# Attention output read back with channels on partitions, and the two norms after it on pairs of tiles

## The reference

```
out = softmax(q k^T / 4) v                 # per head; reshaped to 4096 x 256
y   = out @ Wo.T + bo
x2  = x + layernorm(y)
xn2 = layernorm(x2)                        # mean and variance over 256 channels, eps 1e-5
d2  = sum(xn2^2) + sum(centroid^2) - 2 xn2 @ centroid.T    # 8 experts
w, sel = top_k(sqrt(d2), 2); w = softmax(w)
```

## Time and profile before

| | us |
|---|---|
| median of 3 runs | 1725.83 (1725.29 to 1733.98) |
| the profiled execution, whole | 1724.6 |
| its span, first to last instruction | 1722.8 |
| output stage, 871.8 to 1008.3 | 136.5 |
| routing and start of the experts, 1008.3 to 1061.2 | 52.9 |

### The profile page before, as it was taken

How to read it: one execution, slowest core, us unless ns; L and a number is a source line. 1 busy time by engine, 2 the same in 40 slices (tenths; PEclk the granted TensorE clock), 3 DMA queues, 4 the chain that set the end, 5 groups by cost and what they waited for, 6 DMA issues and landing times.

```text
span 1722.8 us, 33008 instructions
## 1 busy us (share of the span) xinstructions
PE 1522.0 (88%) x9922; PEld 865.8 (50%) x9923; DVE 1204.5 (70%) x2083; ACT 886.8 (51%) x1828; POOL 333.1 (19%) x411
## 2 busy tenths in 40 slices
PE   6887999999999999999988935999999999999900
PEld 3554333333333333333356723777777777777700
DVE  7998989999999999999024666444444444445426
ACT  2333058888888888888845732222222222222226
POOL 5665100000000000000011213222222222222204
PEclk9998579999999999999978956999999999999955
DMA  4474704434444433330533371011011011011072
GB/s 131 133 202 141 135 8 91 104 76 81 67 83 67 99 62 83 58 74 15 162 114 112 120 258 42 31 33 33 30 33 33 30 33 33 30 33 33 27 250 98
DMA packets 113495, 141.44 MB, mean 82 GB/s; under 512 B 36057, under 2 KB 86978, under 8 KB 113410
## 3 DMA queue, kind: packets, MB, share of 16 engines
q1 hardware_dynamic: 106594, 121.68, 28.1%
q0 software_dynamic: 6816, 18.62, 3.3%
HBM read 90.46 MB, written 49.81 MB: 81 GB/s over the span
## 4 chain that ended last, share of the span: by engine, by line
PE 73%; DVE 5%; ACT 3%; DMA 3%; issue 3%; SPq 2%; DVEq 0%; POOL 0%; ACTq 0%; POOLq 0%
PE psum L1449 19%; PE psum L1303 18%; PE psum L1329 16%; PE psum L1468 11%; PE psum L1459 3%; DMA weights<-ot_scr 2%; PE psum L1315 2%; DVE mx L813 2%; ACT work L1145 1%; PE psum L1393 1%; ACT weights L1155 1%; SPq L582 1%; PE psum L1435 1%; PE psum L1378 1%; PE psum L1391 1%
## 5 line engine op out<-in xcount | busy, mean ns | idle before, releaser
L813 DVE TENSOR_REDUCE mx<-psum 128x1 f32<-128x1024 f32 x512 | 625.1, 1222 | 22.4 <-PE psum L1303 18.7
L1145 ACT ACTIVATE work<-psum 128x512 f32<-128x512 f32 x1024 | 556.7, 597 | 131.6 <-PE psum L1315 68.4
L1303 PE MATMUL psum<-stack 48*128 48x512 f32 x1024 | 395.8, 470 | 5.6 <-DVE mx L813 3.7
L1315 PE MATMUL psum<-stack 50*128 50x512 f32 x1024 | 377.3, 448 | 0.0
L1449 PE MATMUL psum<-weights,values 128*128 x1136 | 340.8, 453 | 0.6 <-DVE values L1011 0.6
L1329 PE MATMUL psum<-work,values 128*32 128x256 f32 x4096 | 328.9, 393 | 9.2 <-ACT weights L1155 9.2
L1303 PEld LDWEIGHTS psum<-stack 48*128 48x128 f32 x1024 | 160.8, 197 | 231.0 <-DVE mx L813 199.1
L1449 PEld LDWEIGHTS psum<-weights,values 128*128 128x128 f32 x1136 | 211.2, 191 | 99.5 <-issue 3.0
L1221 ACT ACTIVATE values<-values 128x342 f32<-128x342 f32 x142 | 69.3, 488 | 252.9 <-DVE values L1021 252.9
L1468 PE MATMUL psum<-weights,work 114*128 (+1 forms) x852 | 195.9, 379 | 0.8 <-ACT work L1231 0.8
L1329 PEld LDWEIGHTS psum<-work,values 128*32 128x32 f32 x4096 | 82.1, 108 | 197.5 <-ACT work L1145 102.0
(11 more groups left out here) (173 smaller groups left out, 1425.8 us busy)
## 6 DMA issues: line engine op xcount, KB each, us to landing
stack<-qk_scr SPq DMA_DIRECT2D x192, 128.0 KB, 6.5
qk_scr<-weights SPq DMA_DIRECT2D x8, 2048.0 KB, 7.1
weights<-in_w SPq DMA_DIRECT2D x8, 1368.0 KB, 6.1
ot_scr<-weights SPq DMA_DIRECT2D x16, 512.0 KB, 3.1
weights<-ot_scr SPq DMA_DIRECT2D x32, 256.0 KB, 2.9
weights<-y_d SPq DMA_DIRECT2D x16, 512.0 KB, 8.9
weights<-in_w SPq DMA_DIRECT2D x8, 684.0 KB
work<-in_b SPq DMA_DIRECT2D x8, 684.0 KB, 5.8
```

The source lines that it names most:

```text
L813: dve.tensor_reduce(mx[:, r, a, t:t + 1], bank(4 + 2 * a, 2), AX, ALU.max, negate=True).then_inc(s_max, 1)
L1145: act.activation(pt[u % 4][:, j, :], bank((c + HG * u + n) % 3), ACT.Exp, scale=SC).then_inc(s_exp, 1)
L1303: ins = pe.matmul(bank(4 + 2 * a + half), qs[t3][at:at + QROWS, r, P * t:P * (t + 1)], ks[t3][at:at + QROWS, r, 512 * half:512 * (half + 1 ...
L1315: pe.matmul(bank((t3 + HG * u + n) % 3), ks[t3][at:at + MROWS, r, P * st:P * (st + 1)], qs[t3][at:at + MROWS, r, 512 * half:512 * (half + ...
```

## The change

The stage is worked in 16 pairs of tiles (u = 0 to 15) instead of 32 tiles, and in 4 batches b for the attention output. `load_ot(b)` now reads the values of a batch with channels on partitions and tokens on columns, and the sums, which DRAM holds 16 times, into a second half of the same shape: 32 transfers of 16 partitions x 1024 columns, 64 KB each, 2 MB per batch. VectorE inverts the sums in place, in two halves of 2 x 512 columns on 128 partitions (`invert_sums`), and GpSimd multiplies (`norm_o`). This tile is at once the left operand of `project_o`, so `turn_ot`, `turn_on` and their copies are gone. The two norms handle a pair per step: the small operations take two columns at once, statistics and normalisations remain two instructions, `add_y` and the copy of the transposed `xn2` become one of 512 columns. `squares` is gone; two VectorE operations of 32 columns in the routing work the sum of squares out from variance and inverse deviation.

Loads move as the buffers do. Batches 0 and 1 are loaded late in groups 7 and 11 of the attention (counted from 0), 2 and 3 behind `keep(0)` and `keep(4)`. Wo and the centroids are loaded at group 5; expert 4's first weights move from group 1 to the end of the stage. After `s_slot` there are now two loads, the second weights of expert 3 (684 KB) and then the first weights of expert 7 (1368 KB), where there was one (expert 5, 1368 KB).

```diff
+        ot = [c.take([2, KC, T]) for _ in range(2)]
+        c.at = (E - 1) * KC * 2 * HID
         o_stage = c.take([T])
...
+        c.at = w1_size + 3 * KH * C + C
         w_o, b_o = c.take([KC, C]), c.take([C])[0:1, :]
+        mv_a, mv_b = c.take([NT, 2]), c.take([NT, 2])
+        sd_a, sd_b = c.take([NT, 1]), c.take([NT, 1])
+        rd_a, rd_b = c.take([NT, 1]), c.take([NT, 1])
+        off_a, off_b = c.take([NT, 1]), c.take([NT, 1])
+        st_a, st_b = c.take([2, 2, 6]), c.take([2, 2, 6])
+        assert c.at <= w1_size + 4 * KH * C
+        c = Carve(work)
+        c.at = 16384 - 4 * C
+        yn = [c.take([2, C]) for _ in range(2)]
+        c = Carve(values)
+        xn2 = [c.take([2, C]) for _ in range(2)]
+        xn2_t = [c.take([2, KC, P]) for _ in range(2)]
+        zeros = sb("zeros", [P, C])
...
+        def load_wo(sp):
+            sp.dma_start(w_o, wo.rearrange("(k p) n -> p k n", p=P)).then_inc(s_wo, 16)
+            sp.dma_start(b_o, bo.rearrange("(a n) -> a n", a=1)).then_inc(s_wo, 16)
+            sp.dma_start(cent_t[:, :].rearrange("p (k e) -> p k e", k=KC),
+                         cent.rearrange("(k p) e -> p k e", p=P)).then_inc(s_wo, 16)
+        def load_ot(sp, b):
+            sp.wait_ge(s_ot, 16 * HG * (b + 1))
+            if b >= 2:
+                sp.wait_ge(s_op, 4 * (b - 1))
+            for g in range(HG):
+                src = ot_scr[HG * b + g, :, :].rearrange("(j s d) t -> s j d t", s=2, d=D)
+                for part in range(2):
+                    for j in range(HG):
+                        at = 64 * (g % 2) + D * j
+                        sp.dma_start(ot[b % 2][at:at + D, part, g // 2, :], src[part, j]).then_inc(s_otl[b % 2], 16)
...
-                if g < 2:
-                    load_w1(sp, 3 + g)
+                if g == 0:
+                    load_w1(sp, 3)
+                elif g == 5:
+                    load_wo(sp)
+                elif g in (7, 11):
+                    load_ot(sp, (g - 7) // 4)
...
-            def load_ot(n, p):
-                if isinstance(n, int) and n == 2:
-                    store_o(sp, NG - 1)
-                if isinstance(n, int) and n == 4:
-                    sp.wait_ge(s_ot, 16 * NG)
-                    sp.dma_start(w2_sb[KP:KP + 1, :, 0, :], b2.rearrange("(a e) n -> a e n", a=1)).then_inc(s_w2, 16)
-                if isinstance(n, int) and n in (4, 6, 8, 10):
-                    load_w2(sp, n // 2 - 2)
-                after(sp, s_t1, n - 1)
-                src = ot_scr[bass.ds((n // TPB) * HG, HG), :, bass.ds((n % TPB) * P, P)]
-                sp.dma_start(ot[p], src.rearrange("g p t -> p g t")).then_inc(s_otl[p], 16)
-            def keep(n, p):
-                sp.wait_ge(s_xn2, n + 1)
-                sp.dma_start(xn2_d[bass.ds(n * P, P), :], xn2[p][:, :]).then_inc(s_keep[p], 16)
-                if isinstance(n, int) and early <= NT - 1 - n < E:
-                    load_b1(sp, NT - 1 - n)
-            steps(sp, NT, [(9, keep), (0, load_ot)])
-            sp.wait_ge(s_x2, NT)
+            store_o(sp, NG - 1)
+            sp.dma_start(w2_sb[KP:KP + 1, :, 0, :], b2.rearrange("(a e) n -> a e n", a=1)).then_inc(s_w2, 16)
+            def keep(u):
+                sp.wait_ge(s_xn2, 2 * u + 2)
+                sp.dma_start(xn2_d[2 * P * u:2 * P * (u + 1), :].rearrange("(a p) c -> p a c", p=P), xn2[u % 2]).then_inc(s_keep[u % 2], 16)
+            for u in range(NT // 2):
+                keep(u)
+                if u in (0, 4):
+                    load_ot(sp, 2 + u // 4)
+                if 6 <= u < 11:
+                    load_b1(sp, E - 1 + 6 - u)
+                if 11 <= u < 14:
+                    load_w2(sp, u - 11)
+                if u == 13:
+                    load_w1(sp, E - 4)
+            sp.wait_ge(s_x2, NT // 2)
             sp.dma_start(x2_d.rearrange("(n p) d -> p n d", p=P)[:, kept:, :], x2[:, kept:, :]).then_inc(s_x2s, 16)
-            load_w1(sp, E - 2)
-            sp.wait_ge(s_dot, NT)
-            load_w1(sp, E - 1)
+            sp.wait_ge(s_op, NT // 2)
+            for e in range(E - 3, E - 1):
+                load_w1(sp, e)
...
+            load_w2(sp, 3)
+            load_w1(sp, E - 1)
...
-            def add_y(n, p):
-                if isinstance(n, int) and n == 0:
+            def add_y(u):
+                if u == 0:
                     pool.wait_ge(s_x2l, 64)
-                pool.wait_ge(s_yn, n + 1)
-                pool.tensor_tensor(row(x2, n), row(x2, n), yn[p], ALU.add).then_inc(s_x2, 1)
-            steps(pool, NT, [(6, add_y)])
+                pool.wait_ge(s_yn, 2 * u + 2)
+                both = x2[:, 2 * u:2 * u + 2, :]
+                pool.tensor_tensor(both, both, yn[u % 2], ALU.add).then_inc(s_x2, 1)
+            def norm_o(b):
+                for half in range(2):
+                    pool.wait_ge(s_rs, 2 * b + half + 1)
+                    dims, sums = [ot[b % 2][:, part, :, 512 * half:512 * (half + 1)] for part in range(2)]
+                    pool.tensor_tensor(dims, dims, sums, ALU.mult).then_inc(s_div, 1)
+            norm_o(0)
+            norm_o(1)
+            for u in range(NT // 2):
+                if u in (6, 10):
+                    norm_o(u // 4 + 1)
+                add_y(u)
...
-            def invert_sums(n, p):
-                dve.wait_ge(s_t1, n + 1)
-                v = bank(p).rearrange("p (h c) -> p h c", c=32)
-                dve.reciprocal(o_sum[:, p, :].rearrange("p (h c) -> p h c", c=1), v[:, :, D:D + 1]).then_inc(s_rs, 1)
-            def norm_o(n, p):
-                dve.wait_ge(s_rs, n + 1)
-                after(dve, s_t2, n - 1)
-                v = bank(p).rearrange("p (h c) -> p h c", c=32)
-                dve.tensor_tensor(on[p].rearrange("p (h d) -> p h d", d=D), v[:, :, 0:D],
-                                  o_sum[:, p, :].rearrange("p (h c) -> p h c", c=1).to_broadcast([P, H, D]),
-                                  ALU.mult).then_inc(s_on, 1)
...
+            def invert_sums(b):
+                dve.wait_ge(s_otl[b % 2], 16 * 2 * HG * HG * (b // 2 + 1))
+                for half in range(2):
+                    sums = ot[b % 2][:, 1, :, 512 * half:512 * (half + 1)]
+                    dve.reciprocal(sums, sums).then_inc(s_rs, 1)
+            def stats_y(u):
+                dve.wait_ge(s_op, u + 1)
+                after(dve, s_ya, 4 * (u - 1))
+                for a in range(2):
+                    dve.bn_stats(st_a[:, u % 2, a, :], bank(4 + u % 2)[:, C * a:C * (a + 1)]).then_inc(s_ya, 1)
+            def means_y(u):
+                for a in range(2):
+                    dve.wait_ge(s_ya, 4 * u + a + 1)
+                    dve.bn_aggr(mv_a[:, 2 * u + a, :], st_a[:, u % 2, a, :]).then_inc(s_ya, 1)
...
+            invert_sums(0)
+            invert_sums(1)
+            for u in range(NT // 2 + 1):
+                if u in (6, 10):
+                    invert_sums(u // 4 + 1)
+                if u < NT // 2:
+                    stats_y(u)
+                    means_y(u)
+                if u > 0:
+                    stats_x2(u - 1)
+                    means_x2(u - 1)
+                if u < NT // 2:
+                    invert_y(u)
+                    offset_y(u)
+                if u > 0:
+                    invert_x2(u - 1)
+                    offset_x2(u - 1)
...
+            inverse = rd_b.rearrange("p n a -> p (n a)")
+            step(dve.tensor_tensor(sq[:, :], inverse, inverse, ALU.mult))
+            step(dve.scalar_tensor_tensor(out=sq[:, :], in0=mv_b[:, :, 1], scalar=float(C), in1=sq[:, :],
+                                          op0=ALU.mult, op1=ALU.mult))
...
+            def norm_y(u):
+                act.wait_ge(s_oa, u + 1)
+                after(act, s_x2, u - 1)
+                for a in range(2):
+                    n = 2 * u + a
+                    act.activation(yn[u % 2][:, a, :], bank(4 + u % 2)[:, C * a:C * (a + 1)], ACT.Identity,
+                                   bias=off_a[:, n, :], scale=rd_a[:, n, :]).then_inc(s_yn, 1)
...
+            def save_xn2t(u):
+                act.wait_ge(s_t3, u + 1)
+                after(act, s_dot, u - 1)
+                act.activation(xn2_t[u % 2].rearrange("p a k t -> p (a k t)"), bank((7, 3)[u % 2]), ACT.Copy).then_inc(s_xn2t, 1)
+            for u in range(NT // 2 + 2):
+                if u < NT // 2:
+                    deviation_y(u)
+                if u > 1:
+                    save_xn2t(u - 2)
+                if 0 < u < NT // 2 + 1:
+                    deviation_x2(u - 1)
+                if u < NT // 2:
+                    norm_y(u)
+                if 0 < u < NT // 2 + 1:
+                    norm_x2(u - 1)
...
-            def turn_ot(n, p):
-                pe.wait_ge(s_otl[p], 8 * (n + (2 - p)))
-                after(pe, s_on, n - 1)
-                for k in range(HG):
-                    last = pe.transpose(bank(p)[:, P * k:P * (k + 1)], ot[p][:, k, :], ident[:, :])
-                last.then_inc(s_t1, 1)
...
```

(31 more changed lines are left out.)

183 lines of the change are left out of this document (51 added, 132 removed).

## The result

The changed kernel takes 1800.5 us (median of 4 runs, 1777.3 to 1807.1) against 1726.1 for the kernel before. The ratio is 1.034, 95% interval 1.023 to 1.045; it leaves out the two of the four runs that were over 1.5% above the fastest (1804.3 and 1807.1), and with the medians of all runs it would be 1.043. The forecast was 1748, range 1731 to 1775. The direction was right; the loss is three times the forecast one.

What follows compares the result with a forecast made beforehand. The prediction held the 136.5 us output stage bound by late loads first, then by TensorE. It added 21 (stage) + 0.5 (routing) + 2 (load after routing) = 23.5 us to 1724.6, giving 1748, range 1731 to 1775.

Steps and rivals of the forecast that it cites:

- The start of the stage: Output stage: last constant at 879.3, GpSimd's 1024-column product 2.5 us, project_o(0) at 881.8 at half clock.
- The loop of a pair: Output stage: projection, transposes, copy, deviation and normalisations form a loop of 5.9 us per pair, 9.5 at half clock.
- The inversion: VectorE's reciprocals of sums: 8.4 us per 1024 numbers, 16.8 per batch; batches 2 and 3 cost the stage 28.4 us.
- The clock: TensorE in the output stage: full clock returns after two slow pairs at the start and after each stall; 13.5 us.
- rival (B): TensorE in the output stage: as the main forecast, but the clock doesn't return; 1764 or 1784 us, chance 0.20.
- Sum for the stage: Output stage: end at 987.5 + 28.4 + 13.5 = 1029.4 against 1008.3, so 21 us later.
- the new order: Output stage worked in pairs without the removed transposes: 21 us shorter without anything else, ending at 987.5.
- The transfers in the attention: Sync engine's queue, groups 7 and 11: 32 issues push load_stacks back by 8.9 us, at cost 0.
- my signs: Whole kernel: the forecast is wrong if reciprocals are near 1 or 4 us, pairs go at 4.6, or attention is longer.
- `keep(1)` behind the 32 issues: Output stage: keep(1) stands behind batch 2's issues and norm_x2(3) waits for its buffer; 1 us.
- The start of the experts: After s_slot: 684 KB go ahead of 1368 KB; put at 2 us, between 0 and half of 6.1 us.
- `keep(15)` before the routing: End of the output stage: this store must land before the routing writes into its place; 0 to 2 us.

Runs made afterwards that it cites:

- e3_bias: The changed kernel with the bias added by a product over 128 rows instead of one row; 1768.1 us, ratio to before 1.026.
- e4_w2: The changed kernel with expert 3's second weights loaded ahead of the routing, small statistics in their own tile; 1776.6 us, ratio to before 1.035.
- e2_keep: The changed kernel with loads of batches 2 and 3 issued in pieces behind keep(1) to keep(3) and keep(5) to keep(8); 1803.1 us, ratio to before 1.047.
- e10_nobias: The changed kernel without the bias product, so its output is off; 1756.7 us, ratio to before 1.017.
- e8_pairs: The changed kernel with 8 wide loads per batch, 128-row bias, batches 2 and 3 inverted by pairs, expert 3's second weights before the routing; 1761.5 us, ratio 1.023.
- e7_copy: The changed kernel with 8 wide loads per batch, 128-row bias, and a copy in place of the inversions of batches 2 and 3; 1768.2 us, ratio 1.025.
- e1_attn: The changed kernel with loads of batches 0 and 1 spread 8 per group over groups 7 to 14; 1769.6 us, ratio to before 1.028.

## Why the prediction was wrong, point by point

- **The start of the stage: right.** Last constant 3.7 us after the first (905.2 to 908.9), products of 1024 columns 2.34 us (put at 2.5), `project_o(0)` at 911.45, 6.2 us after the first constant, as worked out.
- **The loop of a pair: right.** Half clock: 9.07 us, put at 9.5. Full clock: 5.13 in `e3_bias`, put at 5.9, but 0.6 of the difference is its other form of the bias; after itself has no stretch of pairs at full clock. TensorE waits 1.08 us in each for `norm_y`, as the loop says. The copy, the deviation and the changes of engine took some 0.9 us in all rather than 1.1.
- **The inversion: the size was off.** 6.51 us for 1024 numbers, between my bounds of 6.4 and 11.3, but at their low end: it is the slope from width 1 to 32, 6.1 ns, that held. My 8.1 ns came from subtracting a guess for PSUM from the row of 16. A batch takes 12.96 us, put at 16.8. That it would be a full stall was right in after: VectorE ran it with nothing between. The estimate of 8.5 us from the Trainium skill (VectorE: DVE Perf Modes, "First, the fixed hardware budget") was no better; the measurement decides.
- **The clock: the step that failed in the stage.** I let it return after two pairs at the start and after each stall (13.5 us in all, "I take two pairs"). It never did for longer than a few us at a time; the price of the one-row bias is 35.2 us, by `e3_bias`, of which some 26 are the clock by the estimate above. I had it as rival (B), but for another reason, gaps in the loop. `e3_bias` speaks against that reason: its TensorE had a longer gap in each pair (1.08 us, 0.36 in after) and was busy for 16.55 of 22 us at clock 1.00, while after was busy for 25 of 25 at 0.50. For the same reason the rule of the Trainium skill (TensorE: Matmul & The Clock Gate, "A second HAM failure mode: psum-queue depth-cycling") on cycling through banks isn't what happened, though the clock did swing (0.50, then 1.00 from 938 to 940, then 0.50 again). What I missed stood in the earlier trace rows: over a third of TensorE's time in a projection is in matmuls of one row. In the kernel before transposes of 128 rows stood between them, six more in each tile than now, and the clock was at 1.00 from 920 to 993; that it was so because of them is argued, as no run takes them away alone.
- **Sum for the stage.** Put: -21 for the new order, +28.4 for the inversions, +13.5 for the clock, in all +20.9. Measured: +36.1. In `e3_bias`, where the clock falls at the stalls and comes back, as my terms have it, the stage is 0.9 longer than before; with the 9 us for the form of the bias that is about +10. So my terms together were some 11 us too high, and 7.7 of it is the inversions (2 x 12.96 instead of 2 x 16.8). The clock that stays low adds some 26 on top; that the two errors partly cancel is luck. The gain of the new order, put at 21, isn't measured by itself.
- **The transfers in the attention: the step that failed outside.** "Cost 0; if this cover were gone, a few us, twice." The cover that I worked out was that of the stack loads, and it did hold: they were pushed back by 9.8 us, put at 8.9, and TensorE didn't wait for them. I didn't ask what else passes through that queue: the store of the maxima, the wait for it, and `store_o` behind it, with a single buffer ahead of it. The cost was 12 us, twice. In the other kernels that kept the 32 issues it was between 3.7 (`e4_w2`, second block) and 20.9 us (`e2_keep`, second block). That a longer attention would prove me wrong was among my signs.
- **`keep(1)` behind the 32 issues: seen, its size not.** Put at 1 us. It was issued at 952.7 and landed at 955.0, where the chain goes through it; but at half clock VectorE and ScalarE had slack, and moving the issues (`e2_keep`) made it worse. What it costs alone isn't known.
- **The start of the experts.** Put at 2 us with 3 as upper bound; it was 7.0. The bound was half of one load's 6.1 us, but the load of 1368 KB behind that of 684 KB landed only after 12.96 us; without the 684 KB ahead of it (`e4_w2`) the experts started 7.2 us earlier. Why 684 KB cost more than the 1368 KB behind them isn't shown.
- **`keep(15)` before the routing.** Put at 0 to 2 us. TensorE's last product ended at 1069.5 and the routing began at 1073.5; the store took 8.21 us to land (1.8 for the last one before), with a load of 1368 KB issued 6.6 us ahead of it in the same queue. Some 4 us.

(The sum itself has a slip of 1.2 us: 1724.6 + 23.5 is 1748 for a profiled execution, and 1749 for the median.)

Where the 72.2 us went: 23.4 blocks of loads, 35.2 the one-row bias in the stage (some 26 by the clock, some 9 by its own length), 0.9 all else in it, 7.0 start of the experts, 5.7 what is left, most of it the clock's return at the attention's start.

## What to carry to other kernels

When loads are moved into a stage that seems to have room, list everything that passes the queue behind them in that stage, the smallest store first, and follow it to the buffer that it frees; room for the loads says nothing on these. Count both the time of the issues and that of the bytes: fewer and larger transfers made it worse here. Where a bias is added by a matmul of one row, try it over all 128 rows, above all when transposes between such matmuls are taken away: it gave 13 us or more of the whole time in each of the four kernels that were tried both ways here (for after by the ratios, 1.034 and 1.026). For a price outside the widths that a trace shows, take the slope over the widest pair of rows.

## What the runs showed of the hardware

- Projections in which two of six matmuls have one row left the granted clock at 0.50 with TensorE busy for 25 of 25 us (after); with 128 rows, or without these two, it was at 1.00 in the stretches from 922 (`e3_bias`) and from 925 (`e10_nobias`), the first matmul being at 917.2 and 918.1.
- At one clock, the matmuls behind a bias product of 256 columns started 0.63 us behind it with one row and 0.43 with 128 rows (1.00), and 1.15 and 0.98 us (0.50).
- A reciprocal in f32 took 6509 ns for 128x1024 and 3345 ns for 128x512 (`e8_pairs`), 6.2 ns for each further column; a copy of 128x1024 took 686 ns (`e7_copy`).
- 32 loads of 64 KB took 15.56 us to issue and landed 2.2 us after their issues; 8 loads of the same 2 MB took 8.24 us to issue, but the 12 issues that followed then took 13.63 us of the queue instead of 5.56.
- A store of 16 KB landed 10.5 us after its issue with 12 loads of 128 KB issued in the 6.1 us ahead of it (after), and 4.4 us with these 10.3 us ahead (before).
- The same code ran at different clocks in two kernels (0.50 in `e1_attn` and 1.00 in `e4_w2` from 240 to 244), with no cause that the traces show.
